# A pair's weighted sums in one burst of 24 matmuls, in a ring of four banks

## What is computed

```python
A1 = einsum('bhqd,bhkd->bhqk', Q1, K1) * scaling
A2 = einsum('bhqd,bhkd->bhqk', Q2, K2) * scaling
attn = softmax(A1) - lam * softmax(A2)
O = einsum('bhqk,bhkd->bhqd', attn, V)
O = O / sqrt(mean(O * O) + EPS) * rms_scale * (1 - LAMBDA_INIT)
out = einsum('bne,de->bnd', O, Wo)
```

## Time and profile before

| what | value |
|---|---|
| median of 3 runs | 2938.79 us (2938.79 to 2944.8) |
| the profiled execution | 2946.47 us, its span 2944.7 us |
| granted TensorE clock, mean | 0.981 |
| PE busy | 2752.8 us (93%) |
| DVE busy | 2317.6 us (79%) |
| ACT busy | 2126.2 us (72%) |
| POOL busy | 1801.3 us (61%) |

### The profile page before, as it was taken

One profiled execution on the slowest core, in us unless ns is written; L12 is line 12 of the kernel. 1 busy time (PEld: TensorE's weight loads), 2 busy tenths in 40 slices (PEclk: granted clock), 3 DMA queues, 4 the chain that ended last, 5 costly groups with the idle time before them and its releaser, 6 DMA issues.

```text
span 2944.7 us, 46590 instructions
## 1 busy us (share of the span) xinstructions
PE 2752.8 (93%) x16447; PEld 2032.8 (69%) x16447; DVE 2317.6 (79%) x4143; ACT 2126.2 (72%) x4692; POOL 1801.3 (61%) x1357
## 2 busy tenths in 40 slices
PE   6999999999899999999999999999999999999996
PEld 3333333333347777788888888888888888888885
DVE  8888888888937877789788777777777778777876
ACT  2677777777766555677877777777777787777773
POOL 3442524332015555677788777788778787777773
PEclk8899999999989999999999999999999999999997
DMA  1000000000022111000000000000000000000000
GB/s 41 7 7 7 12 7 7 7 7 2 2 76 75 48 48 58 8 1 1 1 1 3 3 1 3 3 1 3 3 1 3 3 1 3 3 1 3 3 3 6
DMA packets 25689, 34.83 MB, mean 12 GB/s; under 512 B 4136, under 2 KB 14952, under 8 KB 25456
## 3 DMA queue, kind: packets, MB, share of 16 engines
q1 hardware_dynamic: 25456, 31.85, 3.4%
HBM read 29.08 MB, written 2.23 MB: 11 GB/s over the span
## 4 chain that ended last, share of the span: by engine, by line
PE 67%; DVE 15%; ACT 8%; issue 6%; POOL 5%; DMA 0%; DVEq 0%; POOLq 0%; ACTq 0%
PE P L1798 18%; PE P L1666 9%; PE P L1825 8%; PE P L1809 6%; PE P L1651 5%; PE P L1727 5%; PE P L1639 4%; ACT a_PT L784 4%; DVE c_nm L1376 4%; DVE c_DT L1401 3%; PE P L1781 3%; PE P L1738 2%; PE P L1835 2%; PE P L1629 2%; POOL d_tn L1099 2%
## 5 line engine op out<-in xcount | busy, mean ns | idle before, releaser
L1376 DVE TENSOR_REDUCE c_nm<-P 128x1 f32<-128x1024 f32 x512 | 624.4, 1220 | 303.9 <-PE P L1798 301.9
L908 ACT ACTIVATE c_P<-P,c_nm 128x1024 f32<-128x1024 f32 x512 | 573.0, 1119 | 251.8 <-DVE c_nm L1376 247.5
L1221 DVE TENSOR_REDUCE a_mx<-P 128x1 f32<-128x512 f32 x1024 | 640.2, 683 | 99.5 <-PE P L1639 95.4
L784 ACT ACTIVATE a_PT<-P 128x512 f32<-128x512 f32 x1024 | 537.1, 603 | 165.4 <-PE P L1651 165.2
L2048 POOL TENSOR_TENSOR c_P<-c_P,c_P 128x1024 f32<-128x1024 f32 (+1 forms) x256 | 623.0, 2434 | 21.3
L2046 POOL TENSOR_SCALAR c_P<-c_P,c_rr 128x1024 f32<-128x1024 f32 (+1 forms) x256 | 300.9, 1176 | 338.4 <-DVE c_rr L1388 338.4
L1825 PE MATMUL P<-c_DT,c_xkh 128*128 128x256 f32 x2048 | 451.7, 283 | 24.7 <-DVE c_Yl L1409 23.0
L1651 PE MATMUL P<-a_Qs,a_Ks 32*128 32x512 f32 x1024 | 344.2, 493 | 59.6 <-ACT a_PT L784 53.2
L1825 PEld LDWEIGHTS P<-c_DT,c_xkh 128*128 128x128 f32 x2048 | 350.2, 189 | 37.0 <-DVE c_Yl L1409 29.2
L1798 PE MATMUL P<-c_xth,c_Th 128*128 128x512 f32 x1024 | 365.1, 437 | 2.8 <-ACT c_P L908 2.8
L1401 DVE TENSOR_TENSOR c_DT<-P,c_DT 128x512 fp32r<-128x512 f32 x512 | 348.4, 681 | 9.0 <-ACT c_DT L919 8.8
(11 more groups left out here) (245 smaller groups left out, 5393.6 us busy)
## 6 DMA issues: line engine op xcount, KB each, us to landing
b_cwB<-cw_scratch SPq DMA_DIRECT2D x64, 256.0 KB, 5.0
c_stg<-in_cw SPq DMA_DIRECT2D x8, 640.0 KB, 4.0
a_Qs<-a_mT SPq DMA_DIRECT2D x256, 2.0 KB
b_stg<-in_moe SPq DMA_DIRECT2D x9, 384.0 KB, 3.0
out<-xres SPq DMA_DIRECT2D x15, 128.0 KB, 1.8
xres<-in_x SPq DMA_DIRECT2D x3, 512.0 KB, 7.6
xres<-in_x SPq DMA_DIRECT2D x2, 256.0 KB, 3.0
a_hTl_f<-in_wqk SPq DMA_DIRECT2D x1, 512.0 KB, 3.6
```

What stands on the lines that cost most here:

```text
L784: e.activation(m.PT[j][hs % 4][:, :], bank("scores", u, hs, j), ACT.Exp, scale=SCALE).then_inc(m.S["a_exp"])
L908: e.activation(m.P1[s][n % 4][:, :], P[:, k:k + 2, :].rearrange("p c k -> p (c k)"), ACT.Exp, bias=m.nm[:, n % 4, s:s + 1], accum_out=m.sm ...
L1221: e.tensor_reduce(m.mx2[u % 2][:, t // 4, j, t % 4, half:half + 1], bank("maxima", u, t, j, half), AX, ALU.max).then_inc(m.S["a_max_dve"])
L1376: e.tensor_reduce(m.nm[:, n % 4, s:s + 1], P[:, k:k + 2, :].rearrange("p c k -> p (c k)"), AX, ALU.max, negate=True).then_inc(m.S["c_nm"])
```

## The change

The four quarters become one step of 24 matmuls, issued with odd tau n = 2p + 5, half 1, after `output`, where the second quarter was. The fourth stood with the tau after it. The step takes a bank of the ring, and bank 6 joins the ring, which then has four. The step waits for the second half of the pair's `low` before its first matmul. The waits that named part 3 now name the whole step. Nothing else is touched.

```diff
-    "pv": lambda p, part: {"c_pv": 1, "c_yh": 1, "c_yl": 1} if part == 3 else {},
+    "pv": {"c_pv": 1, "c_yh": 1, "c_yl": 1},
...
-    "pv": lambda p, part: [("c_yl", "pv", p, 3)],
+    "pv": lambda p: [("c_yl", "pv", p)],
...
-    ring.slots, ring.i = [4, 5, 7], 0
+    ring.slots, ring.i = [4, 5, 7, 6], 0
...
-            if 5 <= n < NTAU + 5:
-                pair, part = (n - 5) // 2, 2 * ((n - 5) % 2) + s
-                if part == 0:
-                    p.on([6], "pv", pair, part)
-                else:
-                    p.do("pv", pair, part)
+            if s and 5 <= n < NTAU + 5 and n % 2:
+                on_ring("pv", (n - 5) // 2)
...
-    def pv(p, part):
-        if part == 3:
-            w.wait_ge(*at("c_pv", "pv", p, 3))
-            if p > 1:
-                w.wait_ge(*at("c_og", "output", 2 * p - 3))
-            e.activation(m.Yh[p % 2][:, :], P[:, 6, 0:256], ACT.Copy).then_inc(m.S["c_yh"])
+    def pv(p):
+        w.wait_ge(*at("c_pv", "pv", p))
+        if p > 1:
+            w.wait_ge(*at("c_og", "output", 2 * p - 3))
+        e.activation(m.Yh[p % 2][:, :], bank("pv", p)[:, 0:256], ACT.Copy).then_inc(m.S["c_yh"])
...
-    def pv(p, part):
-        b, half = p // 32, part // 2
-        w.wait_ge(*at("c_dl", "low", 2 * p + 1, half))
-        w.wait_ge(*at("c_dl", "low", 2 * p, 1))
-        if b:
-            w.wait_ge(*at("c_xTl", "keep_x", b, half))
-        else:
-            w.wait_ge(*at("c_xTl", "keep_x", 0, None, i=1 + half))
-        if part == 0:
-            bank("pv", p, 0)
-        for i in range(2):
-            kt = 2 * part + i
-            for j, (x, l) in enumerate(((m.xkh, 0), (m.xkl, 0), (m.xkh, 1))):
-                tt = e.matmul(P[:, 6, 0:256], x[:, 128 * kt:128 * kt + 128], m.DT[p % 2][l][:, kt, :],
-                              start=(kt == 0 and j == 0), stop=(kt, j) == (7, 2))
-        if part == 3:
-            tt.then_inc(m.S["c_pv"])
+    def pv(p):
+        b = p // 32
+        ps = bank("pv", p)
+        w.wait_ge(*at("c_dl", "low", 2 * p + 1, 1))
+        for half in range(2):
+            if b:
+                w.wait_ge(*at("c_xTl", "keep_x", b, half))
+            else:
+                w.wait_ge(*at("c_xTl", "keep_x", 0, None, i=1 + half))
+            for kt in range(4 * half, 4 * half + 4):
+                for j, (x, l) in enumerate(((m.xkh, 0), (m.xkl, 0), (m.xkh, 1))):
+                    tt = e.matmul(ps[:, 0:256], x[:, 128 * kt:128 * kt + 128], m.DT[p % 2][l][:, kt, :],
+                                  start=(kt == 0 and j == 0), stop=(kt, j) == (7, 2))
+        tt.then_inc(m.S["c_pv"])
```

More of the change, by code:

```diff
@@ L878, in keep_x @@
         if b:
-            w.wait_ge(*at("c_pv", "pv", 32 * b - 1, 3))
+            w.wait_ge(*at("c_pv", "pv", 32 * b - 1))
         else:
@@ L915, in turn @@
         if p > 1:
-            w.wait_ge(*at("c_pv", "pv", p - 2, 3))
+            w.wait_ge(*at("c_pv", "pv", p - 2))
         for t in b_free(v):
@@ L1402, in low @@
                         ALU.subtract).then_inc(m.S["c_dl"])
-    def pv(p, part):
-        if part == 3:
[L1406 to L1410, removed]
+    def pv(p):
+        w.wait_ge(*at("c_yh", "pv", p))
+        if p > 1:
+            w.wait_ge(*at("c_og", "output", 2 * p - 3))
+        e.tensor_tensor(m.Yl[p % 2][:, :], bank("pv", p)[:, 0:256], m.Yh[p % 2][:, :].bitcast(F32),
+                        ALU.subtract).then_inc(m.S["c_yl"])
     def factor(u, first, end):
@@ L1810, in turn, with pv @@
         tt.then_inc(m.S["c_tr"])
-    def pv(p, part):
-        b, half = p // 32, part // 2
-        w.wait_ge(*at("c_dl", "low", 2 * p + 1, half))
-        w.wait_ge(*at("c_dl", "low", 2 * p, 1))
-        if b:
-            w.wait_ge(*at("c_xTl", "keep_x", b, half))
-        else:
-            w.wait_ge(*at("c_xTl", "keep_x", 0, None, i=1 + half))
-        if part == 0:
-            bank("pv", p, 0)
-        for i in range(2):
-            kt = 2 * part + i
-            for j, (x, l) in enumerate(((m.xkh, 0), (m.xkl, 0), (m.xkh, 1))):
-                tt = e.matmul(P[:, 6, 0:256], x[:, 128 * kt:128 * kt + 128], m.DT[p % 2][l][:, kt, :],
-                              start=(kt == 0 and j == 0), stop=(kt, j) == (7, 2))
-        if part == 3:
-            tt.then_inc(m.S["c_pv"])
+    def pv(p):
+        b = p // 32
[11 more added lines that the diff above has]
+        tt.then_inc(m.S["c_pv"])
     def output(n):
         h, p, qs = n // 2 % 8, n // 2, slice(128 * (n % 2), 128 * (n % 2) + 128)
-        w.wait_ge(*at("c_yl", "pv", p, 3))
+        w.wait_ge(*at("c_yl", "pv", p))
         ps = bank("output", n)
```

## The result

The changed kernel takes 2936.1 us (median of 20 executions, 2923.9 to 2948.5), the kernel before 2945.0 (20, 2938.4 to 2959.9): a ratio of 0.9973, 95% interval 0.9960 to 0.9985. It is faster, by 0.27%; forecast were 2916 us and 0.78%. The 2936.1 lie in the band that the prediction gave to no difference (2934 to 2944), though the gain is clear of noise. The profiled execution takes 2927.33 us (span 2925.5, mean clock 0.985), 19.1 less than the profiled one of before.

What follows compares the result with a forecast made beforehand. TensorE sets the pace in the second attention. Of 5.9 us waited a round 4.5 stay: 20 us gained, plus 1 in the first thirty taus and 1 at the end, make 2924 profiled, 2916 as median; range 2866 to 2958.

Steps and rivals of the forecast that it cites:

- its walk: Step-by-step timing of an ordinary pair after the change: 12.35 us, no wait, on the edge.
- what would show it: Signs expected in the profile after: transpositions' waits under 30 places, some 40 us of scores waiting, VectorE's `Yh` wait about 200.
- The conditions for being wrong: `c_P` waits of 0.3 or more before every odd second score (slower), or hardly any (far faster).
- The first rival, ACT's order: Slower, chance 0.18: exponents behind a held `Yh`, without cover on the even tau; about 35 us lost, 2974.
- the second, that all waits go: Faster, chance 0.12 for all or most waits gone: 83 us less, 2856.
- the bank waits: Steady stretch before: transpositions waiting for a ring bank, 34.4 us, and sums for bank 6, 22.6 us; expected to lose their cause.
- the knot: Taus 14 to 16: VectorE late; TensorE lost 1.9 us at bank 6 and 1.5 at the next transposition.
- The steady rounds: Rounds of 16 taus from tau 30 on: 1.4 us gained in each, 20 us over 14.1 rounds.
- the clock: Slower, chance 0.05: a wait over 3 us at tau 15 would slow TensorE's clock each round; 35 us, 2950.
- The first thirty taus: Start of the second attention, half of it without FFN products: 1 us gained.
- The end: Last `Yh` issued a tau earlier, against 1.4 us more behind the last `low`: 1 us gained.
- the last step of the forecast: From profiled execution to median of runs: the 7.7 us difference of the kernel before, taking 2924 to 2916.

Runs made afterwards that it cites:

- the second experiment: Changed kernel with the burst kept in bank 6 and the ring left at banks 4, 5 and 7: 3029.8 us, ratio 1.0290 to the kernel before.
- halves: Changed kernel with the 24 matmuls in two steps of 12, both on the odd tau: 2918.8 us, ratio 0.9909 to the kernel before.
- the filled kernel: Changed kernel with tau 15's second transposition step making its transpositions six times over (20 more, same output): 2919.1 us, ratio 0.9909 to the kernel before.
- group three: Runs timed together on one chip: kernel before 2944.3 us, changed kernel without edit 2933.5 us, ratio 0.9965.
- the third time: Changed kernel without edit, profiled once more: profiled execution 2933.5 us, span 2931.8 us.

## Why the prediction was right in its walk and wrong in its size

**Right.** The sign, and most of what was named under what would show it: the transpositions' wait fell from 96 places to none in the steady stretch, no sums wait for `c_Yl`, scores wait for `c_P` 39.2 us (forecast some 40), most at tau 15 and then tau 3 (tau 1, named too, has 0.1), VectorE's wait for `Yh` rose to 134 (forecast 200), 24 sums take 2.86. The conditions for being wrong were not met either. The first rival, ACT's order, needed a mean wait of 0.74 a pair; it is 3.7 / 8 = 0.46, and none in ordinary pairs. Of the second, that all waits go, the bank waits went and the knot stayed. The Trainium skill's sentence on repeated gaps (Perfetto Trace Analysis, Identifying Performance Opportunities) holds for the gaps themselves, as the second experiment measured; what it gives no price for is the work that lay between two takers. The Trainium skill's other sentence, on smaller pieces (the same page, Optimizing Scalar/DVE Operations), speaks of those engines' own instructions; for TensorE's burst, halves were a draw.

**The steady rounds.** Forecast: 4.5 left of 5.9, 20 gained. Measured waits a round: 0.93 at tau 3 (1.05), 0.13 at tau 11 (0.2), 0.1 at tau 1 (0.9), none to speak of in ordinary pairs (0.45), 2.5 at tau 15 (1.9): 3.7. The 0.8 over 14 rounds is 11 more, and the two slow stretches of before, 3, go too: 34 without slow stretches, and the filled kernel measures 35.2 less than before (1456.8 for 1491.9). That the two agree is partly luck: the sum leaves out the 7 that the changes of batch cost, and waits of 0.1, which stand at about six places of a round before and at four after. The 3.7 hide errors as well: tau 15 came out longer, tau 1 and the ordinary pairs shorter.

**In the sum, the term that failed is the clock, put at nothing.** It was a rival priced only for a wait "over 3", because the one row with a fallen clock stood behind a pause of 3.6. The wait came out at 2.5, and behind six of thirteen that was enough: 9.7 of the 35.2 us went back. It should have been a term of the sum with a share of rounds, since pauses of 1.9 at bank 6 had already let the clock fall twice in before. One of the two, the wait and the work behind it (the other stands at 2563.8):

```profile
1807.90:1812.90 5.00, 3.24 (x22) 2.63 (x21) 4.96 (x6) 2.78 (x8) 4.92 (x3) 1.00 0.00 2
1812.90:1816.30 3.40, 3.40 (x12) 2.76 (x11) 2.65 (x8) 1.70 (x3) 0.93 (x2) 0.50 0.00 0
```

The Trainium skill (TensorE: Matmul & The Clock Gate, HAM oscillation) tells of a longer wait, for a DMA, that returns with each tile and slows the clock each time; in this trace the pause of 2.4 to 2.8 us does so 6 times in 13.

**Two small terms had the wrong sign.** The first thirty taus: 1 gained forecast, 5.0 lost, because the taus with `turn_weights`, where VectorE is late and the quarters had covered for it, were not walked. The end: 1 gained forecast, 0.9 lost; TensorE ran at half clock from 2893.5 us, in before from 2915.4, and the last `Yl` waited 3.15 (1.77):

```profile
2893.50:2910.60 17.10, 8.13 (x30) 7.10 (x31) 12.98 (x44) 2.10 (x7) 2.91 (x6) 0.50 0.03 8
```

```profile
2889.97 0.43 DVE L1403 TENSOR_TENSOR c_Yl<-P,c_Yh 128x256 fp32r<-128x256 f32 x1 [3.15 <-ACT c_Yh L922]
```

**The 20 us between 2916.0 and 2936.1.** The larger part comes from the last step of the forecast: "the same difference gives 2916", which set the changed kernel's median 7.7 below its profiled execution, as three executions had it before. It lies 8.8 above, 16.5 us off. 6.2 of these are the base: 3 executions gave before a median of 2938.8, 20 give 2945.0. 10.3 are that the medians lie 8.9 apart and the profiled executions 19.1: the profiled execution after is 8.8 below its own median, that of before 1.5 above. The last 3.7 are the sum's, 22.8 forecast and 19.1 between the profiled executions; that this is little is luck, since larger terms above cancel in it.

Why the median after lies above its profiled execution stays open. For the clock: in the 20 executions the five above 2942 us have mean clocks of 0.969 to 0.971, the five under 2930 us 0.974 to 0.985, and in group three the changed kernel's mean over its executions is 0.9745, that of before 0.9819. The kernel with the pause filled spreads over 7.0 us in 4 executions, the changed kernel over 16.2 in 6 of the same group. Against it: the kernel with the `weigh` later keeps the whole pause of tau 15 and spreads over 3.6 in 6. The mean clock doesn't tell where it fell, in the one profile of a slower execution (the third time) 5.0 of 6.2 us lay ahead of the second attention, and none of the executions near 2948 was profiled.

## What to carry to other kernels

Before scattered work is gathered into one burst, list what each piece covered: here 0.71 us between two takers of a bank; without a further bank the kernel lost 83 us by it. When a pause on TensorE grows or is merged from two, add the clock behind it to the price, as a share of the rounds, even where the longest pause seen so far let it fall only now and then; work that does no harm, put into the pause, buys that back. Walk the stretches with other steps in them (the first thirty taus, the changes of batch) as carefully as the steady one. And don't carry the distance between one profiled execution and a median of three from one kernel to another: here that alone was 16.5 of 20 us.

## What the runs showed of the hardware

More matmuls took less time: with 20 more transpositions at each of 13 tau 15s the time from tau 30 to 254 fell by 9.7 us, while the steps there stayed as late and every slow stretch went. How often the clock falls is not a property of the kernel: behind pauses of 2.4 to 2.8 us it fell in 6, 6 and 7 of 13 in three executions, and in 3 of 13 in the kernel with the `weigh` later.

Two small VectorE steps took a quarter and a sixth of their former time without an edit to them. Groups by line and shape, steady stretch, before:

```profile
L1475 DVE SCALAR_TENSOR_TENSOR d_tn<-d_x,d_mx 128x256 f32<-128x256 f32 x13 | 23.2, 1783 | 0.0
...
L1471 DVE TENSOR_SCALAR d_sc<-d_mx 128x16 f32<-128x16 f32 x13 | 13.9, 1066 | 0.0
```

and after:

```profile
L1469 DVE SCALAR_TENSOR_TENSOR d_tn<-d_x,d_mx 128x256 f32<-128x256 f32 x13 | 5.4, 415 | 0.0
...
L1465 DVE TENSOR_SCALAR d_sc<-d_mx 128x16 f32<-128x16 f32 x13 | 2.2, 166 | 0.0
```

1783 ns became 415, 1066 became 166. In before one of POOL's long steps ran beside each of them (L2048 beside the first, L2041 beside the second); in after that step has ended before the first begins, and the second stands where one of POOL's steps ends and the next begins. In the kernel with `xq` later the first takes 1905 ns again, thirteen times of thirteen beside that same step of POOL:

```profile
L1469 DVE SCALAR_TENSOR_TENSOR d_tn<-d_x,d_mx 128x256 f32<-128x256 f32 x13 | 24.8, 1905 | 0.0
```

So the time of the first goes with that step of POOL in three kernels; no edit was aimed at it alone. It is the likely reason why tau 1's 0.9 never came: the forecast had carried the slow durations over.
